# Layer 2's cross attention in two lanes of eight heads, norms applied by ScalarE, biases added by POOL, and a new order of the program

## What is computed

```python
x = x + _L2_xattn_ref(_layernorm(x, axis=-1), ctx_768, L2_xattn_Wq, L2_xattn_bq, ...)
x = x + _L2_attn_ref(_layernorm(x, axis=-1), L2_attn_Wq, L2_attn_Wk, L2_attn_Wv, L2_attn_Wo)
```

## Time and profile before

| | us |
|---|---|
| median of three runs | 3016.06 |
| lowest and highest | 3009.4, 3019.45 |
| the profiled execution | 3007.17 |
| its span, first to last instruction | 3005.9 |

### The profile page before, as it was taken

One profiled execution on the slowest core, in us unless ns is written; L12 is line 12 of the kernel. 1 busy time (PEld: TensorE's weight loads), 2 busy tenths in 40 slices (PEclk: granted clock), 3 DMA queues, 4 the chain that ended last, 5 costly groups with the idle time before them and its releaser, 6 DMA issues.

```text
span 3005.9 us, 65105 instructions
## 1 busy us (share of the span) xinstructions
PE 2475.7 (82%) x28016; PEld 1708.2 (57%) x28016; DVE 1931.9 (64%) x5138; ACT 1224.0 (41%) x1857; POOL 724.4 (24%) x644
## 2 busy tenths in 40 slices
PE   5788988776777987667788888888888887899999
PEld 2555556555555554444667666666655555556665
DVE  6877877676565786677766555554556655666543
ACT  2343333444333226666424434432424544544322
POOL 3322425443111320000012222221100021345343
PEclk8899999899879999798999989987879978899999
DMA  3001323000000010000000000000001000022133
...
DMA packets 50465, 84.70 MB, mean 28 GB/s; under 512 B 9536, under 2 KB 24768, under 8 KB 49792
## 3 DMA queue, kind: packets, MB, share of 16 engines
...
...
## 4 chain that ended last, share of the span: by engine, by line
PE 55%; DVE 21%; ACT 12%; issue 7%; POOL 5%; DMA 0%; SPq 0%; DVEq 0%; POOLq 0%; ACTq 0%
PE psum L831 4%; PE psum L798 4%; PE psum L802 4%; PE psum L401 3%; PE psum L1433 3%; PE psum L2030 2%; PE psum L1443 2%; PE psum L1791 2%; PE psum L1527 2%; DVE c_L3x_most L1568 1%; PE psum L2051 1%; PE psum L1239 1%; ACT c_L2x_p L1826 1%; PE psum L569 1%; ACT c_L2x_p L1824 1%
## 5 line engine op out<-in xcount | busy, mean ns | idle before, releaser
L786 POOL TENSOR_TENSOR c_L3f_h<-c_L3f_h,c_L3f_spread 128x512 f32<-128x512 f32 x96 | 122.1, 1304 | 111.0 <-DMA c_L3f_spread<-scratch 104.1
L821 DVE TENSOR_TENSOR c_L3f_h<-c_L3f_h,psum 128x512 f32<-128x512 f32 (+1 forms) x112 | 75.1, 683 | 87.1 <-PE psum L802 77.7
L1791 PE MATMUL psum<-constants_held,c_L2x_p 128*128 128x128 f32 x512 | 86.6, 325 | 53.1 <-ACT c_L2x_p L1826 53.0
L831 PEld LDWEIGHTS psum<-weights,c_L3f_h 128*128 128x128 f32 (+1 forms) x896 | 108.6, 195 | 17.9 <-issue 15.5
L1791 PEld LDWEIGHTS psum<-constants_held,c_L2x_p 128*128 128x128 f32 x512 | 70.0, 167 | 83.6 <-ACT c_L2x_p L1826 76.1
L811 ACT ACTIVATE c_L3f_h<-psum 128x512 f32<-128x512 f32 (+1 forms) x112 | 64.8, 595 | 129.1 <-PE psum L798 129.0
L798 PE MATMUL psum<-c_L3f_xT,weights 128*128 128x512 f32 (+1 forms) x224 | 115.4, 604 | 2.3 <-DVE c_L3f_h L821 2.3
L802 PE MATMUL psum<-c_L3f_xT,weights 128*128 128x512 f32 (+1 forms) x224 | 114.2, 598 | 0.5 <-ACT c_L3f_h L811 0.4
L831 PE MATMUL psum<-weights,c_L3f_h 128*128 128x128 f32 (+1 forms) x896 | 112.1, 281 | 0.0
L786 POOL TENSOR_TENSOR c_L0f_h<-c_L0f_h,c_L0f_spread 128x512 f32<-128x512 f32 x64 | 79.1, 1270 | 112.7 <-DMA c_L0f_spread<-scratch 109.5
L1852 DVE TENSOR_REDUCE c_L2x_mx<-psum 128x8 f32<-128x1024 f32 x64 | 77.9, 1217 | 33.3 <-PE psum L1433 32.6
...
## 6 DMA issues: line engine op xcount, KB each, us to landing
...
```

The lines of the kernel that those rows point to most:

```text
L786: nc.gpsimd.tensor_tensor(h, h, j.m["spread"][:, f, :], ALU.mult).then_inc(*j.up("mixed"))
L831: put = nc.tensor.matmul(j.psum[:, 0, k * P:(k + 1) * P], j.m["h"][0:rows, f, k * P:(k + 1) * P], j.weight("down")[0:rows, f * P:(f + 1) * ...
L1791: put = t.transpose(psum[:, n // 4, (n % 4) * P:(n % 4 + 1) * P], m["p"][:, n * P:(n + 1) * P], j.c["ident"])
```

## The change

**L2x in lanes.** `pe_L2x`, `act_L2x` and `dve_L2x` keep the head and tail of a job; the tiles move into six generators, `pe_lane_L2x(h)`, `act_lane_L2x(h)` and `dve_lane_L2x(h)` for h = 0 and 1, each with letters of its own in `ORDER` (m, n, x, y, w, z). Lane h has heads 8h to 8h + 7, row groups 2h and 2h + 1 of PE, and banks 2h and 2h + 1 only: scores and transposes in both, values' product in 2h, the turned output in 2h + 1. Its scores of tile w + 1 wait for its own division of tile w. The eviction of the product (128x256 in place of 128x512), the reciprocal (128x8) and the division (128x64) are now two instructions a tile, one for each lane; scores are two batches of 4 matmuls in place of one of 8.

**Keys and biases.** In L2x, POOL makes copies 2 and 3 of `kx` by `tensor_tensor` on 128x1024 (`pool_L2x`); DVE keeps 0 and 1. In L1a, L2x and L3x the bias is added to x by POOL (`pool_bias`), 24 adds of 128x512.

**Norms.** In the early programs of all blocks DVE computes in place of the four applications one small `shift` = -mean x rstd (128x4 or 128x2, 160 in all), and ACT applies the norm as `Identity(rstd * x + shift)`, 128x128 at a time (128x96 for L1x's context): 544 instructions (`act_norm`, L395, letter k). The second norms of L0a and L3a stay on DVE.

**Order.** `PLAN` is the same; `ORDER` is another string from start to end. The activation table loads that the compiler puts into ACT's list are 129 after 121.

```diff
-def dve_norm_twice(nc, j, out, x, once=None):
+def dve_shift(nc, j, i, shift, moments, root):
+
+    nc.vector.wait_ge(*j.at("rstd", i))
+    nc.vector.scalar_tensor_tensor(shift, moments[:, :, 0], -1.0, root, ALU.mult, ALU.mult).then_inc(*j.up("shift"))
+
+
+def act_norm(nc, j, i, out, x, root, shift):
+
+    nc.scalar.wait_ge(*j.at("shift", i))
+    for t in range(x.shape[1]):
+        put = nc.scalar.activation(out[:, t, :], x[:, t, :], ACT.Identity, bias=shift[:, t:t + 1], scale=root[:, t:t + 1])
+    put.then_inc(*j.up("normed"))
...
+def pool_bias(nc, j, bias):
+
+    j.begin(nc.gpsimd)
+    nc.gpsimd.wait_ge(*j.at("normed", 1))
+    nc.gpsimd.tensor_tensor(j.x, j.x, bcast(j.weight(bias), 1, j.tiles), ALU.add).then_inc(*j.up("biased"))
...
+def pe_lane_L2x(h):
+
+    groups = (2 * h, 2 * h + 1)
+
+    def program(nc, j):
+        t, m, psum = nc.tensor, j.m, j.psum
+        for w in range(j.tiles):
             yield
-            t.wait_ge(*j.at("exp", 2 * w + half + 1))
-            for n in range(8 * half, 8 * half + 8):
+            if w:
+                t.wait_ge(*j.at(lane_name("att", h), w))
+            else:
+                t.wait_ge(*j.at("q_ready", 1))
+                t.wait_ge(*j.at("va", 1))
+                t.wait_ge(*j.at("kx", 2))
...
+def pool_L2x(nc, j):
+    g, m = nc.gpsimd, j.m
+    yield
+    g.wait_ge(*j.at("k_ready", 1))
+    for n in (2, 3):
+        put = g.tensor_tensor(m["kx"][:, n, :], m["kT"][:], j.c["lane4"][:, n:n + 1].to_broadcast([P, 8 * SC]), ALU.mult)
+    put.then_inc(*j.up("kx"))
+    yield
+    pool_bias(nc, j, "bo")
...
 ORDER = (
-    "DDdvDVddlLDdqQqQppddDDdaPapaggAGlPApppvDPAvdavPPLGPvVVAvVVDVVDdddppaapagglDDvdPAppPpAQqPALGGPPPvvavvVVvAppVaapaVdddVDDvD"
...
+    "QqdddvDDDVlLDKdkdpDDddDlpdaakQqgLPpagPAApppPDAvvaGPPvGPvvVVKApapadVpaVVddPpPgvglAAGdVkppvPAGPPPvavVvQqVAvVppagVvVVapddDD"
```

409 lines of the change are left out of this document (236 added, 173 removed).

## The result

The changed kernel takes 3032.4 us (median of four runs, 3030.8 to 3036.7) against 3016.3; the ratio is 1.0071, with a 95% interval of 1.0042 to 1.0101. By the ratio it is slower by 21 us, by the two medians by 16, where the prediction had it faster by 57, and it lies outside the range of 2912 to 3020. The profiled execution took 3036.67 us, its span 3035.4.

A forecast was written before the change was run, and what follows sets the result against it. No engine was full; L2x (342 us) was mostly held by each tile's chain across engines. From 3007 us profiled, -52 in L2x and -5 elsewhere gave 2950, or 2959 against the 3016 median; own range 2938 to 2980, overall 2912 to 3020.

The forecast's parts named there:

- Step 2: In L2x on PE, 24 extra batches of score matmuls at 1.11 us add 27 us, from 234.5 to 261.
- Step 3: In L2x, PE's granted clock might rise from 0.88 to 0.94, turning 261 us of PE work into 244.
- Step 4: In L2x, half-width evictions (26 us for 18) and applied norms (9 us) raise ACT from 229.5 to 246 us.
- Step 5: In L2x, DVE falls from 233.5 to about 220 us: key copies, norms, biases leave; halved divisions and shifts add.
- Step 6: L2x goes from 342 to 290 us, -52, taking 252 us of PE at a fill of 0.87; bounds -69 to -3.
- step 1: In L2x, a lane's tile chain takes 10.3 us, a context 197 us, so the bound passes to the fullest engine.
- Step 7: Two key copies on POOL start each L2x job 0.9 us later, hidden: 0; uncovered +4, by port exclusion +10.
- Step 8: Outside L2x, norms moved from DVE to ACT gain only through queues: -5 us together, bounds +20 and -40.
- the bound passes to PE at its low clock: Lanes leave PE broken up, clock stays: L2x -17 us, key copies +9, elsewhere +5; 3013, no change; chance 0.12.
- ACT as gate: ACT's norms delay PE's turn at job heads, 0.8 us for 90 of 136 groups: +72 against -57, 3031; chance 0.13.
- other blocks that moved by more than 25 us each: Sign of being wrong: all blocks other than L2x together moving by more than 25 us either way.
- PE's wait ahead of the turns: Sign of being wrong: PE waiting for ACT before the turns of the normed x for over 30 us in all.

## Why the prediction was wrong, step by step

The steps name L2x by two windows: the prediction's 342 us end at 1449 us, the 352 above at the last product, and the 356 after answer to the 352. So changes are compared with changes here.

- *Step 2, extra batches:* 27 us on PE, measured 28.7. Right, but I put it on PE's sum only, as if the stage were bound by sums. In a bad place in the lists 40 us of it cost 52; in the new order, with lanes alone, 28 us of it left L2x at most 8 us longer.
- *Step 3, the clock:* 0.94 expected in L2x, 0.85 measured. Wrong in sign. More busy time did not bring the clock up.
- *Step 4, ACT in L2x:* a rise of 16.5 us to 246, measured 11, from 234.5 to 245.8; that the sum itself was met is luck of the windows. A norm's piece took 481 ns where I took 320 and called 417 an upper bound, though in a row they overlap (24 pieces, 9.8 us busy); the evictions took 367 ns for 400.
- *Step 5, DVE in L2x:* a fall of 13.5 us to 220, measured 5, from 239.4 to 234.6. The miss is the key copies, 14 x (1763 - 747) = 14 us above what was counted; the other terms came out lower than counted.
- *Step 6, the stage: this is the step that failed.* I had one mean, 0.69, for the 342 us of L2x, and lifted it to 0.87, the fill of a block with other work, since four lanes would lift the bound of the chain: -52 us, measured +4. Two things were wrong in it. First, a quarter of L2x is job changes, 19 to 27 us each. PE is busy for 0.81 of them already, and lanes do nothing for them (89.5 us before, 89 with the lanes alone), so only the tiles could give anything. Second, the tiles did not give it, though 91 of PE's 108 idle us lie there: a pair's took 65 us from first to last scores for 66.5, where three rounds of a lane's own chain are 31 us by step 1. With the lanes alone and no extra batch, L2x fell by 10 us in the profile and the whole by 8, not by 52. That four short chains do not run side by side because each of the three engines takes its pieces in a fixed row is my reading; the runs that leave work out of ACT and DVE fit it, and no run frees the lists. In the changed kernel PE's idle time in L2x did fall, by 29 us, and its busy time rose by 33 (steps 2 and 3): the fill came to 0.78 with nothing gained.
- *Step 7, key copies:* 0 counted, 4 uncovered, 10 by the rule of the Trainium skill, SBUF — State Buffer, "Who interferes with whom". Measured 13 in both orders, in the old one together with the biases, and with copies that last as by that rule, 4.79 us where 5.5 were worked out. It should have been a term of the sum.
- *Step 8, norms elsewhere:* -5. By the run with the norms alone DVE was relieved by 139 us and not 182 - 29 = 153, ACT loaded with 205 and not 174 + 10 = 184. The number can't be told by itself: it is -24 to -28 in the new order, +58 to +164 in the old. My bounds of -40 and +20 did not hold the latter. Together, order, norms and biases make +17 over the lanes alone (1.0028 against 0.9972). That the order is another one everywhere stood in the prediction as something the rows say nothing of; it had no term in the sum, and it alone is worth 41 us where only the lanes are changed.
- *The rivals:* "the bound passes to PE at its low clock" was nearest in its mechanism, with a clock of 0.85 and PE's busy time taking what the idle time gave, but had -17 us in L2x for +4. "ACT as gate" has the right number, 3031, for a reason that the changed kernel's trace does not bear out: 6.9 us of waiting at the turns. It is what the same edit does in an order that was not made for it.

Of the prediction's own signs of being wrong, three showed: L2x over 315 us, DVE's key copies far over 0.75 us, and other blocks that moved by more than 25 us each (L2f -32, L3x +41). PE's wait ahead of the turns did not.

The sum as the runs have it: lanes -8, keys on POOL +13, order with norms and biases +17, together the 21 us measured, but for rounding. They have to come out so, since each term is the difference of neighbouring runs; it is no check. What stays open: how much of the +17 is the batches standing apart in the new order (with lanes alone L2x is only 1 to 8 us longer there), the 15 us that L2a lost (77 to 79 us in the old order with norms on DVE, 92 to 94 in all five profiles with the new one there), or L3x; and why the clock is lower in L3x in the new order.
